# Routing constants moved into the attention, the block table beside the digit search, the list written out, expert weights prepared one half ahead

## The chip, the cores and the metric

One core of one Trainium2 chip runs the whole program. The metric is device time in microseconds (us) from one launch to its end, the median of three runs. The engines are named as the profile names them: PE (TensorE), DVE (VectorE), ACT (ScalarE), POOL (GpSimd) and SP (SyncE, which only issues DMAs here).

## What is computed

The input x has 16 batches of 512 tokens with 256 values each. An attention layer with 8 heads comes first, then a mixture of experts. Cut to what matters here:

```python
x = x + ga * attn(layernorm(x) * (1 + ca) + sa)      # 16 x 512 x 256
h = layernorm(x) * (1 + cb) + sb
logits = h @ Wr + br                                  # 8192 tokens x 8 experts
top_vals, top_idx = top_k(logits, 2)
w = softmax(top_vals)
cap = 1280                                            # tokens that an expert takes
kv, ki = top_k(where(flat_idx == e, w_flat, -1e30), cap)   # for each expert e
tok, gate = flat_tok[ki], w_flat[ki] where valid else 0
y = gelu(h[tok] @ W1[e] + b1[e]) @ W2[e] + b2[e]      # 256 -> 1024 -> 256
out = zeros.at[tok].add(y * gate)
x = x + gb * (layernorm(out + h) * gamma + beta)
```

With the inputs given, the bias of the router outweighs the rest of the logits, so all tokens choose the same two experts. Each of these takes 1280 tokens, which is 5 blocks of 256, and 10 blocks are computed in all.

## The kernel before

Three parts follow one another. `attention` runs over the 16 batches with a hand-made order of the work of each batch (`body(b, par)` with 32 slots `n`; batches -2 and -1 are the run-in). It ends with LOGITS, 128 x 64 x 8.

`route` begins behind a barrier. POOL makes constants one after the other, each with a wait for the one before (`link`, L1103 to L1149). DVE finds the two best experts of every token (L1243 to L1268) and writes KEY; PE turns KEY into one row for each expert and sixteenth of the tokens (L1201, 4 transposes). DVE then waits for POOL's last constant before L1276. The threshold of each expert is searched in ten digits of base 8 (`digit`, L1282): DVE counts four candidates (JUNK, L1286) and ACT three (L1168), PE adds the counts over the partitions with SAME (L1206), and DVE picks the digit (L1297, L1300). Behind the digits DVE marks the chosen tokens and gives each its place in the expert's list (GT L1317 to DST L1336). It counts the blocks of each expert (L1339 to L1343), PE transposes DST (L1215), and DVE works out the table INFO of active experts, blocks and first blocks on one partition in some 20 small operations (L1348 to L1368). Only then it turns the places into row and column (D L1373 to AF L1382), for both choices of each token at once. SP reads INFO and loads W1F and W2F, 1 MB each, of the first expert (L1193, L1194).

The list itself is built in 16 steps of 8 token columns. DVE makes two one-hot tiles, OE (8 x 80) and OB (8 x 128); POOL multiplies five of the eight parts of OE by token numbers into OA (L1155), ACT the other three (L1176); PE adds OB times OA into one bank of PSUM (L1228). OE, OA and OB have two buffers, and the steps are a hardware loop of two. At the end DVE makes IDX, the list of tokens (L1398 to L1401).

`experts` runs, on each engine, a loop over the active experts and an inner one over their blocks (`each`, L1493). At its head each engine reads the number of experts, the expert, its blocks and its first block from INFO into registers. For every block POOL gathers 256 rows of `h_rows` into XG with two indirect DMAs (L1548) and scatters the result of an earlier block (L1435). PE transposes XG (L1661), DVE splits it into a high and a low part XTH and XTL (L1604, L1606), PE multiplies by W1 (`mm1`), ACT takes the GELU (L1587), DVE splits that into HH and HL, and PE multiplies by W2 (`mm2`); all products are three passes (high x high, high x low, low x high; L92 to L94). The gather of block g+1 is released by the transposes and by NEXT (L1614) of block g, and the transposes of g+1 stand behind `mm1(g, 4)` in PE's order. At the head of each expert ACT writes the high parts W1H and W2H (L1576, L1579), and DVE the low parts W1L (L1618), ahead of NEXT and the split of the tokens, and W2L (L1622) behind them. SP loads the next expert's W1F once W1L is there and its W2F once W2L is there (L1516, L1518).

`last_norm` reads the sums back, normalises and writes the output. The change only adds one wait for it on SP.

## Time and profile before

| | |
|---|---|
| median of three runs | 1386.81 us (1386.51 to 1387.3) |
| the profiled execution | 1389.0 us |
| its span, first to last instruction | 1387.2 us |
| PE busy | 1163.1 us, 84% of the span |
| DVE busy | 995.6 us, 72% |
| POOL busy | 971.6 us, 70% |
| ACT busy | 754.9 us, 54% |
| mean granted clock of PE | 0.909 of full speed |

```profile
## 2 busy tenths in 40 slices
PE   7899999999999999999999999999931164979500
PEld 5556566665656666565666656565431163979500
DVE  3888687777767777776777778676457884777596
ACT  4565666666576666657666665665413233444144
POOL 3386978878697887869788786978743066545268
PEclk9999999999999999999999999999965555999855
```

Each digit stands for 34.7 us. The first 29 or 30 are the attention, the next four the routing, the next four or so the experts, and the last three the final normalisation. How to read the rows further down: in the timeline the first column is the start in us from the span's start, the second the duration; "x8" means that eight instructions are merged, and the brackets at the end give how long the engine sat idle before and who ended that. "SPq" and "POOLq" are the queues of these engines, where instructions that are not counted as work stand.

### The profile page before, as it was taken

The numbers are of one execution on the slowest core, as the hardware profiler recorded it, in microseconds if no ns is written. First come the engines' busy times: TensorE is split into PE (matmuls) and PEld (weight loads), VectorE is DVE, ScalarE is ACT, GpSimd is POOL, SyncE is SP. The second block draws the span as 40 slices with busy tenths as digits, with TensorE's granted clock in tenths as the row PEclk, the third lists the DMA queues.
The fourth block names the chain that finished last, engine by engine and source line by source line (L and its number), as shares of the span: only waits on it lengthen the run. The fifth ranks groups of instructions, "written<-read, shape, count | busy, mean of one in ns | idle before, by whom it ended". The sixth has DMA issues, their size and how long they took to land. (4 is left out here: it accounts for less than half of the span.)

```text
span 1387.2 us, 23869 instructions
## 1 busy us (share of the span) xinstructions
PE 1163.1 (84%) x5973; PEld 783.3 (56%) x5974; DVE 995.6 (72%) x2205; ACT 754.9 (54%) x1482; POOL 971.6 (70%) x1081
## 2 busy tenths in 40 slices
PE   7899999999999999999999999999931164979500
PEld 5556566665656666565666656565431163979500
DVE  3888687777767777776777778676457884777596
ACT  4565666666576666657666665665413233444144
POOL 3386978878697887869788786978743066545268
PEclk9999999999999999999999999999965555999855
DMA  4000101011010101101010100001032013232474
GB/s 149 16 18 16 58 6 62 16 47 46 15 53 8 62 16 46 46 15 53 9 62 16 46 32 17 32 17 46 31 129 24 18 43 88 43 95 43 87 253 166
DMA packets 68477, 70.89 MB, mean 51 GB/s; under 512 B 12912, under 2 KB 64032, under 8 KB 68272
## 3 DMA queue, kind: packets, MB, share of 16 engines
q1 hardware_dynamic: 46800, 47.18, 10.7%
q10 hardware_dynamic: 16896, 16.78, 3.6%
q0 software_dynamic: 4704, 6.11, 2.9%
q8 instruction: 23, 0.38, 0.1%
q14 instruction: 54, 0.44, 0.1%
HBM read 40.35 MB, written 29.45 MB: 50 GB/s over the span
## 5 line engine op out<-in xcount | busy, mean ns | idle before, releaser
L559 ACT ACTIVATE PF<-PS 128x512 f32<-128x512 f32 x512 | 298.3, 595 | 256.8 <-PE PS L929 247.6
L821 DVE TENSOR_REDUCE NMAX<-PS 128x1 f32<-128x512 f32 x512 | 342.4, 682 | 88.0 <-PE PS L938 84.5
L472 POOL TENSOR_TENSOR SF<-SF,PF 128x512 f32<-128x512 f32 x252 | 322.0, 1300 | 14.7 <-ACT PF L559 14.5
L1010 PE MATMUL PS<-PF,V 128*64 128x512 f32 x1024 | 248.0, 605 | 0.0
L928 PE MATMUL PS<-Q,K 128*128 128x512 f32 x512 | 222.3, 434 | 2.8 <-ACT PF L559 2.8
L938 PE MATMUL PS<-K,Q 128*128 128x512 f32 x512 | 205.5, 403 | 10.6 <-DVE NMAX L821 10.2
L929 PE MATMUL PS<-Q,K 128*128 128x512 f32 x512 | 201.4, 393 | 0.0
L578 ACT ACTIVATE Q<-PS 64x512 fp32r<-64x512 f32 x256 | 151.5, 592 | 48.3 <-PE PS L94 43.3
L469 POOL TENSOR_TENSOR SF<-PF 128x512 f32<-128x512 f32 x126 | 162.0, 1301 | 19.6 <-ACT PF L559 19.6
L500 POOL TENSOR_TENSOR XL<-XF,XH 128x512 fp32r<-128x512 f32 x63 | 82.6, 1312 | 128.5 <-ACT XH L633 128.4
L928 PEld LDWEIGHTS PS<-Q,K 128*128 128x128 f32 x512 | 96.5, 188 | 120.5 <-ACT PF L559 54.6
L668 DVE STREAM_TRANSPOSE XF<-PS 128x512 f32<-128x512 f32 x64 | 45.9, 717 | 119.4 <-PE PS L1028 119.4
L1010 PEld LDWEIGHTS PS<-PF,V 128*64 128x64 f32 x1024 | 62.1, 136 | 110.2 <-issue 93.9
L938 PEld LDWEIGHTS PS<-K,Q 128*128 128x128 f32 x512 | 96.4, 189 | 46.1 <-DVE NMAX L821 21.3
L929 PEld LDWEIGHTS PS<-Q,K 128*128 128x128 f32 x512 | 96.8, 189 | 10.6
L789 DVE TENSOR_TENSOR Q<-PS,Q 64x512 fp32r<-64x512 f32 x128 | 87.5, 683 | 3.7 <-ACT Q L578 1.6
L1587 ACT ACTIVATE HF<-PS,B 128x256 f32<-128x256 f32 x80 | 38.0, 474 | 81.4 <-PE PS L94 69.2
L92 PE MATMUL PS<-GH,XH 128*128 128x256 f32 x256 | 75.8, 296 | 3.5 <-DVE YT L796 2.1
L1155 POOL TENSOR_TENSOR OA<-OE,TOK 128x400 fp32r<-128x400 f32 x16 | 26.7, 1668 | 70.1 <-DVE OE L1390 70.1
L93 PE MATMUL PS<-GL,XH 128*128 128x256 f32 x256 | 72.0, 281 | 0.0
L94 PE MATMUL PS<-GH,XL 128*128 128x256 f32 x256 | 72.0, 281 | 0.0
L1028 PE MATMUL PS<-SF,ONE 128*64 128x512 f32 x252 | 64.8, 592 | 0.0
(327 smaller groups left out, 2519.7 us busy)
## 6 DMA issues: line engine op xcount, KB each, us to landing
X<-in_L_attn_x SPq DMA_DIRECT2D x16, 512.0 KB, 3.4
MODB<-mod_rows SPq DMA_DIRECT2D x16, 512.0 KB, 3.7
h_rows<-H ACTq DMA_DIRECT2D x16, 512.0 KB, 3.0
acc_rows<-H ACTq DMA_DIRECT2D x16, 512.0 KB, 4.1
out_x<-X SPq DMA_DIRECT2D x16, 512.0 KB, 2.9
A<-acc_rows SPq DMA_DIRECT2D x15, 512.0 KB, 8.8
W1F<-in_L_ffn_W SPq DMA_DIRECT2D x3, 1024.0 KB, 4.9
W2F<-in_L_ffn_W SPq DMA_DIRECT2D x3, 1024.0 KB
```

The source lines that it names most:

```text
L92: eng.matmul(out, lhs[0], rhs[0], start=first, stop=False)
L469: s_sum.done(pool.tensor_tensor(total, PF[:, u % 8 - 2, :], tile, ALU.add))
L472: s_sum.done(pool.tensor_tensor(total, total, tile, ALU.add))
L500: s_xlo.done(pool.tensor_tensor(XL[:, p, :], XF[:, :], XH[:, p, :].bitcast(F32), ALU.subtract))
L559: s_exp.done(act.activation(PF[:, u % 8, :], st_bank(u), ACT.Exp))
L578: s_qhi.done(act.activation(Q1[half * R:(half + 1) * R, 2 * idx + odd, :], bank[odd * R:(odd + 1) * R, :], ACT.Copy))
L789: s_qlo.done(dve.tensor_tensor(Q2[0:R, h, :], bank[odd * R:(odd + 1) * R, :], Q1[odd * R:(odd + 1) * R, h, :].bitcast(F32), ALU.subtract))
L821: s_mred.done(dve.tensor_reduce(NMAX[:, p % 2, r:r + 1], mx_bank(u), AX.X, ALU.max, negate=True))
L928: pe.matmul(st_bank(u), K1[:, kp, keys], Q1[:, h, :], start=True, stop=False)
L929: s_st.done(pe.matmul(st_bank(u), K2[:, kp, keys], Q2[:, h, :], start=False, stop=True))
L938: s_mx.done(pe.matmul(mx_bank(u), Q1[:, h, c * P:(c + 1) * P], K1[:, kp, :], start=True, stop=True))
L1010: last = pe.matmul(num_bank(p)[odd * R:(odd + 1) * R, :], V1[:, vp, c, :], PF[:, k % 8, :], start=(c == 0), stop=(c == TC - 1))
```

## The change

- `routing_constants` holds nearly all of POOL's constants. POOL runs it in the attention, in slot 20 of batch -1, before any addition of exponentials. LOWER, ECOLI and ECOL are made by DVE in the attention too (`same_expert`). In `route` POOL makes only ONES, ZT, ZP and BEFORE, and DVE waits for them ahead of KEY.
- The block table is worked out beside the digits: ACT counts the tokens of each expert with one Sign over HI, PE, POOL and ACT make the table on all 128 partitions in small operations, and DVE copies it to INFO in digit 6. POOL's first scatter comes behind the table.
- Behind the digits ACT's Sign takes the place of GT, and RANK (sign and running count in one) lets one comparison with a count give SEL and its sum, so that the addition and the reduction behind SEL go.
- The places are turned into row and column for the first choice of each token first; the work for the second choice (`second`) stands between the first six steps of the list. The steps are written out. ACT copies IOT into PSUM, and OE and OB read it there.
- ACT makes W1H (in two halves) and W2H of the first expert before the list, and of the next one at the end of the last block. DVE makes the first half of W1L before `s_list`, or at the end of an expert's last block, and the second half behind the split of the tokens. PE waits for that half before `mm1(g, 4)`.
- SP waits for the first gather before it loads the second expert's weights. POOL reads the table before it waits for IDX.

```diff
@@ -471,8 +489,58 @@
                     s_sum.wait(pool, b, 2 * (TC - 1) * p + 2 * (c - 2) + odd)
                     s_sum.done(pool.tensor_tensor(total, total, tile, ALU.add))
 
+            def routing_constants():
+
...
+                    n[0] += 1
+                    pool.wait_ge(s_rc, n[0])
+                f32 = dict(allow_small_or_imprecise_dtypes=True)
+                RANK8, IOT, SPARE, TOK1, NEED, NBLEV = (m[x] for x in ("RANK8", "IOT", "SPARE", "TOK1", "NEED", "NBLEV"))
+                LEVEL, STEP, MOVE = (m[x] for x in ("LEVEL", "STEP", "MOVE"))
+                link(pool.iota(RANK8[:, :], pattern=[[-1, E]], base=E, channel_multiplier=0, **f32))
+                link(pool.iota(ECOLI, pattern=[[0, 1]], base=0, channel_multiplier=1))
...
+                for j, blocks in enumerate((0, 0, 2, 3, 4)):
+                    link(pool.memset(NBLEV[:, j:j + 1], float(2 * blocks * BLK - NT)))
+                for d in range(NDIG):
+                    link(pool.tensor_scalar(STEP[:, d, :], SIGN, weight(d), None, ALU.mult))
+                    link(pool.tensor_scalar(LEVEL[:, d, :], COUNT, weight(d), None, ALU.mult))
...
                 for n in range(UNITS):
+                    if isinstance(b, int) and (b, n) == (-1, 20):
+                        routing_constants()
...
+                mask(dve.scalar_tensor_tensor(out=m["LOWER"][:, :], in0=DIFF, scalar=float(P), in1=m["SAME"][:, :],
+                                              op0=ALU.is_gt, op1=ALU.mult))
+                dve.wait_ge(s_rc, 2)
+                mask(dve.tensor_scalar(ECOLI, ECOLI, E - 1, None, ALU.bitwise_and))
+                mask(dve.tensor_scalar(m["ECOL"][:, :], ECOLI, float(CAP), float(-1 - BIG), ALU.mult, ALU.add))
...
+        pool.memset(ONES[:, :], 1.0).then_inc(s_pool, 1)
         pool.memset(ZT[:, :], 0.0).then_inc(s_pool, 1)
         pool.memset(ZP[:, :], 0.0).then_inc(s_pool, 1)
-        pool.memset(ONES[:, :], 1.0).then_inc(s_pool, 1)
-        assert n[0] + 4 == POOL_CONSTS
-        pool.iota(DIFF[:, :], pattern=[[1, P]], base=P, channel_multiplier=-1).then_inc(s_pool, 1)
+        pool.wait_ge(s_pool, ZEROS)
+        pool.memset(BEFORE[:, :], 1.0).then_inc(s_pool, 1)
+        pool.wait_ge(s_pool, ZEROS + 1)
+        pool.affine_select(out=BEFORE[:, :], in_=BEFORE[:, :], compare_op=ALU.is_gt, fill=0.0, base=0,
+                           pattern=[[1, P]], channel_multiplier=-1).then_inc(s_pool, 1)
...
+        pool.wait_ge(s_nba, 1)
+        pool.tensor_scalar(OVER[:, :], NBLEV[:, :], TOTAL[:, :], LOW8[:, :], ALU.is_lt, ALU.mult).then_inc(s_nbp, 1)
+        pool.wait_ge(s_nba, 3)
+        pool.tensor_scalar(PICK[:, :], IOT[:, 0:E], PRIOR[:, 0:1], OVER[:, 0:1], ALU.is_equal, ALU.mult).then_inc(s_nbp, 1)
+        pool.tensor_scalar(LASTB[:, :], BLOCKS[:, :], -1.0, None, ALU.add).then_inc(s_nbp, 1)
+        pool.wait_ge(s_nbp, 3)
+        for j, which in enumerate((PIDX, LASTB, FIRSTB)):
...
+        pool.tensor_scalar(TABLE[:, 3 * E + 1:3 * E + 2], BLOCKS[:, :], 1.0, None, ALU.mult).then_inc(s_nbp, 1)
         first_scatter(pool, m)
...
+        act.activation(iot_ps, IOT[:, :], ACT.Copy).then_inc(s_iot, 1)
...
+        act.wait_ge(s_split, 1)
+        act.wait_ge(s_pool, POOL_CONSTS)
+        act.activation(SGN[:, :], HI[:, :], ACT.Sign, bias=ONES[:, 0:1], accum_out=ASG[:, :]).then_inc(s_asg, 1)
+
+        def blocks(d):
+
+            if d == 1:
+                act.wait_ge(s_nbt, 1)
+                act.activation(TOTAL[:, :], asg_ps, ACT.Copy).then_inc(s_nba, 1)
+            if d == 2:
+                act.wait_ge(s_nbt, 2)
+                act.activation(PRIOR[:, :], prior_ps, ACT.Copy, accum_out=FIRSTB[:, :]).then_inc(s_nba, 1)
+                act.activation(JUNKB[:, :], OVER[:, :], ACT.Copy, accum_out=BLOCKS[:, :]).then_inc(s_nba, 1)
+
...
+        act.activation(SGN[:, :], LOW[:, :], ACT.Sign, bias=CAND[:, NDIG % 2, 0:1], scale=-1.0, accum_out=CNT[:, 1:2]).then_inc(s_sgn, 1)
+        high_weights_1(act, m, 0)
+        high_weights_2(act, m, 0)
+        for j in range(STEPS):
+            act.wait_ge(s_oe, j + 1)
+            for r in range(RPOOL, RING):
+                act.activation(OA[:, j % 2, r, :], OE[:, j % 2, r, :], ACT.Copy,
+                               scale=tok[:, j * RING + r:j * RING + r + 1]).then_inc(s_oact, 1)
...
+            if d == 5:
+                pe.wait_ge(s_nbp, 8)
+                pe.wait_ge(s_nba, 3)
+                pe.matmul(table_ps, ONES[:, :], TABLE[:, :], start=True, stop=True).then_inc(s_nbt, 1)
...
-        dve.wait_ge(s_pool, 1)
...
+        dve.wait_ge(s_pool, POOL_CONSTS)
         for q in range(TC):
             dve.scalar_tensor_tensor(out=KEY[:, q, :, :], in0=EQ[:, q::TC, :], scalar=-1.0, in1=OH1[:, q::TC, :],
                                      op0=ALU.add, op1=ALU.add).then_inc(s_key, 1)
-        dve.wait_ge(s_pool, POOL_CONSTS)
...
+            if d == 6:
+                dve.wait_ge(s_nbt, 3)
+                dve.tensor_copy(m["INFO"][:, :], table_ps[0:1, :]).then_inc(s_info, 1)
...
-        link(dve.tensor_scalar(GT[:, :], LOW[:, :], thr, None, ALU.is_gt, ALU.add, accum_out=CNT[:, 1:2]))
...
+        dve.wait_ge(s_sgn, 1)
+        link(dve.tensor_tensor(CNT[:, 3:4], CNT[:, 2:3], CNT[:, 1:2], ALU.add))
...
+        link(dve.scalar_tensor_tensor(out=RANK[:, :], in0=SGN[:, :], scalar=FAR, in1=SCAN[:, :], op0=ALU.mult, op1=ALU.add))
...
-        link(dve.tensor_tensor(SEL[:, :], SEL[:, :], GT[:, :], ALU.add))
-        link(dve.tensor_reduce(CNT[:, 3:4], SEL[:, :], AX.X, ALU.add))
+        link(dve.tensor_scalar(SEL[:, :], RANK[:, :], CNT[:, 4:5], None, ALU.is_le, ALU.add, accum_out=CNT[:, 5:6]))
...
-        dve.wait_ge(s_nb, 1)
-        eid, nb, cum, act_, cua, z = (NBR[:, j, :] for j in range(6))
-        link(dve.tensor_copy(eid, IOT[0:1, 0:E]))
-        link(dve.tensor_scalar(act_, nb_ps[0:1, :], 0.0, None, ALU.is_gt))
...
-        link(dve.tensor_copy(m["INFO"][:, :], TABLE[:, :]))
-        dve.sem_inc(s_info, 1)
...
+        def second(j):
+
+            if j == 0:
+                link(dve.tensor_tensor(EQ[:, :, :], by_tok, by_expert(D12[:, 0, :]), ALU.is_equal))
+            elif j == 1:
+                link(dve.scalar_tensor_tensor(out=EQ[:, :, :], in0=EQ[:, :, :], scalar=float(BIG), in1=by_tok,
+                                              op0=ALU.mult, op1=ALU.add))
+            elif j == 2:
+                link(dve.tensor_reduce(D12[:, 1, :], EQ[:, :, :], AX.X, ALU.min))
+            elif j == 3:
+                to_integers(1)
+            elif j == 4:
+                to_places(1)
+            elif j == 5:
+                to_floats(1)
...
+        to_integers(0)
+        to_places(0)
+        to_floats(0)
+        dve.wait_ge(s_iot, 1)
+        for j in range(STEPS):
+            dve.wait_ge(s_mm, j + 1)
+            dve.tensor_tensor(OE[:, j % 2, :, :], iot_ps[:, 0:SLOTC].unsqueeze(1).broadcast_to([P, RING, SLOTC]),
+                              af[:, j * RING:(j + 1) * RING].unsqueeze(2).broadcast_to([P, RING, SLOTC]), ALU.is_equal).then_inc(s_oe, 1)
+            dve.tensor_tensor(OB[:, j % 2, :, :], iot_ps.unsqueeze(1).broadcast_to([P, RING, P]),
+                              bf[:, j * RING:(j + 1) * RING].unsqueeze(2).broadcast_to([P, RING, P]), ALU.is_equal).then_inc(s_ob, 1)
+            second(j)
+
+        low_weights_1(dve, m, 0, 0)
...
+def half_of_inner(j):
+
+    return slice(j * (F // 2), (j + 1) * (F // 2))
+
+
+def high_weights_1(act, m, a):
+
+    m["s_w1"].wait(act, a, 0)
+    for j in range(2):
+        cols = half_of_inner(j)
+        m["xs"]["w1h"].done(act.activation(m["W1H"][:, :, cols], m["W1F"][:, :, cols], ACT.Copy))
+
+
+def high_weights_2(act, m, a):
+
+    m["s_w2"].wait(act, a, 0)
+    m["xs"]["w2h"].done(act.activation(m["W2H"][:, :, :], m["W2F"][:, :, :], ACT.Copy))
+
+
+def low_weights_1(dve, m, a, j):
+
+    cols = half_of_inner(j)
+    m["xs"]["w1h"].wait(dve, a, j)
+    m["xs"]["w1l"].done(dve.tensor_tensor(m["W1L"][:, :, cols], m["W1F"][:, :, cols], m["W1H"][:, :, cols].bitcast(F32), ALU.subtract))
...
+        sp.wait_ge(s_gx.sem, 16 * BT)
         with sp.Fori(0, nact) as a:
 
             e = sp.value_load(INFO[0:1, bass.ds(a + 1, 1)], min_val=0, max_val=E - 1)
             k_row, f_row = sp.snap(e * KC), sp.snap(e * FC)
 
-            s_w1l.wait(sp, a, 0)
+            s_w1l.wait(sp, a, 1)
...
-        pool.wait_ge(m["s_idx"], 1)
-        each(pool, None, block, block)
+
+        def first(e, a, g):
+
+            pool.wait_ge(m["s_idx"], 1)
+
+        each(pool, first, block, block)
...
+        def last(e, a, g, k):
+
+            block(e, a, g, k)
+            high_weights_1(act, m, a + 1)
+            s_m2.wait(act, g, FC - 1)
+            act.activation(DUMMY[:, 0:1], IDENT[:, 0:1], ACT.Copy)
+            high_weights_2(act, m, a + 1)
+
+        each(act, None, block, last)
...
         def expert(e, a, g):
-            s_w1h.wait(dve, a, 0)
-            s_w1l.done(dve.tensor_tensor(W1L[:, :, :], W1F[:, :, :], W1H[:, :, :].bitcast(F32), ALU.subtract))
             next_gates(e, g)
             split_tokens(g)
+            low_weights_1(dve, m, a, 1)
             s_w2h.wait(dve, a, 0)
...
+            else:
+                low_weights_1(dve, m, a + 1, 0)
...
+                if f == FC // 2:
+                    s_w1l.wait(pe, a, 1)
                 mm1(g, f)
...
+        nact = sp.value_load(m["INFO"][0:1, 3 * E:3 * E + 1], min_val=1, max_val=E)
+        m["xs"]["w2h"].wait(sp, nact, 0)
```

## Rows read from the trace of the kernel before

**Rows 1.** Stretches, whole chip: us, busy of PE, PEld, DVE, ACT, POOL, then PEclk, DMA.

```profile
0.00:1030.00 1030.00, 996.13 (x4800) 623.35 (x4801) 737.57 (x1534) 626.12 (x1201) 794.21 (x847) 0.99 0.12 37
...
1110.00:1153.00 43.00, 30.83 (x129) 28.70 (x130) 32.91 (x32) 13.85 (x48) 26.69 (x16) 0.50 0.09 32
```

**Rows 2.** Timeline, start of the routing: start, us, engine, line, operation, idle before.

```profile
1030.60 0.69 DVE L1243 TENSOR_REDUCE M<-LOGITS 128x64 f32<-128x512 f32 x1 [0.50 <-POOL RANK L1110]
...
1044.04 1.11 PE L1201 MATMUL PS<-IDENT,KEY 128*128 128x128 f32 x4 [14.17 <-DVE KEY L1268]
...
1048.57 0.69 DVE L1276 TENSOR_SCALAR BITS<-PS 128x512 uint32<-128x512 uint32 x1 [4.58 <-POOL DIFFr L1149]
```

**Rows 3.** Timeline, between the last digit and the list.

```profile
1091.42 0.75 DVE L1318 TENSOR_SCALAR_CACHE_REDUCE EQT<-LOW,CAND 128x512 f32<-128x512 f32 x1
...
1099.12 0.74 DVE L1341 SCALAR_TENSOR_TENSOR CNT<-PS,CNT 128x1 f32<-128x1 f32 x4
...
1100.24 1.12 PE L1215 MATMUL PS<-IDENT,DST 128*128 128x128 f32 x4 [2.57 <-DVEq L1344]
...
1105.55 0.69 DVE L1373 TENSOR_REDUCE D<-PS 128x64 f32<-128x512 f32 x1 [0.15 <-DVE INFO L1368]
...
1110.19 0.82 DVE L1390 TENSOR_TENSOR OE<-IOT,AF 128x640 f32<-128x640 f32 x1 [0.47 <-DVE AF L1382]
```

**Rows 4.** Timeline, one step of the list, and the first instruction behind the last.

```profile
1115.17 0.90 DVE L1390 TENSOR_TENSOR OE<-IOT,AF 128x640 f32<-128x640 f32 x1 [0.49 <-PE PS L1228]
...
1115.99 1.21 DVE L1393 TENSOR_TENSOR OB<-IOT,BF 128x1024 fp32r<-128x1024 f32 x1
...
1116.25 1.67 POOL L1155 TENSOR_TENSOR OA<-OE,TOK 128x400 fp32r<-128x400 f32 x1 [0.86 <-DVE OE L1390]
...
1118.16 1.93 PE L1228 MATMUL PS<-OA,OB 128*128 128x80 f32 x8 [0.61 <-POOL OA L1155]
...
1153.50 0.24 DVE L1398 SCALAR_TENSOR_TENSOR LF<-PS,SPARE 128x80 f32<-128x80 f32 x1 [3.41 <-PE PS L1230]
```

**Rows 5.** Groups of instructions, the last stage: POOL additions of 512.

```profile
L1850 POOL TENSOR_TENSOR X<-X,A 128x512 f32<-128x512 f32 x32 | 39.3, 1264 | 1.1 <-DVE A L1796 1.1
```

**Rows 6.** The chain in order of time, behind the list: start, us, what.

```profile
1154.70 0.52 POOLq L1491
...
1157.50 0.03 POOLq L1502
```

**Rows 7.** Timeline, the first gather.

```profile
1160.35 2.89 POOL L1548 DMA_INDIRECT XG<-h_rows,TOKN  x1 [0.30 <-issue]
...
1162.58 0.38 SPq L1516 DMA_DIRECT2D W1F<-in_L_ffn_W  x1
...
1167.99 1.11 PE L1661 MATMUL PS<-IDENT,XG 128*128 128x128 f32 x4 [14.23 <-DMA XG<-h_rows,TOKN]
```

**Rows 8.** A gather in the middle of an expert: its instruction, and a stretch with PEclk, DMA.

```profile
1220.24 1.12 POOL L1548 DMA_INDIRECT XG<-h_rows,TOKN  x1 [0.30 <-issue]
...
1222.00:1223.00 1.00, 0.96 (x8) 0.86 (x8) 0.87 (x3) 0.04 (x1) 0.18 (x2) 1.00 0.49 135
```

**Rows 9.** Timeline, the second gather.

```profile
1171.66 2.32 POOL L1548 DMA_INDIRECT XG<-h_rows,TOKN  x1 [0.30 <-issue]
...
1173.29 0.37 SPq L1518 DMA_DIRECT2D W2F<-in_L_ffn_W  x1
...
1178.45 0.65 PE L1661 MATMUL PS<-IDENT,XG 128*128 128x128 f32 x4 [2.36 <-DMA XG<-h_rows,TOKN]
```

**Rows 10.** Timeline, between the two experts.

```profile
1236.29 2.29 DVE L1618 TENSOR_TENSOR W1L<-W1F,W1H 128x2048 fp32r<-128x2048 f32 x1 [2.02 <-ACT W1H L1576]
...
1238.51 0.17 DVE L1614 COPY NEXT<-XG 128x2 f32 x1
...
1247.80 0.65 PE L1661 MATMUL PS<-IDENT,XG 128*128 128x128 f32 x4 [1.32 <-DMA XG<-h_rows,TOKN]
```

**Rows 11.** Timeline, POOL in the first batch of the attention.

```profile
50.26 2.53 POOL L469 TENSOR_TENSOR SF<-PF 128x512 f32<-128x512 f32 x2 [19.63 <-ACT PF L559]
```

## What was predicted, and how

> **What bounds the kernel now.** I read the stretches first. Up to 1030 us PE is busy for 996 of 1030 us at a granted clock of 0.99 [rows 1]: that part is bound by PE, and the change touches it at one place only. Behind it no engine is full. In the list, from 1110 to 1153, PE, DVE, POOL and ACT are busy for 31, 33, 27 and 14 of 43 us, and the clock is 0.50, which is 1.2 GHz [rows 1]. There time goes by a chain from engine to engine, so I read the timeline link by link, and at each idle bracket ask what ended it. Five places stand out. DVE sits 4.58 us until POOL's last constant [rows 2]. The table stands between PE's transposes, which end at 1101.36, and D at 1105.55 [rows 3]. OE takes another 4.64 us from D [rows 3]. POOL reads the table from 1154.70 to 1157.50, behind the list [rows 6]. And the first gather takes 7.64 us, from its second instruction at 1160.35 to PE at 1167.99 [rows 7].
>
> **The sum** is made against the profiled execution (span 1387.2 us, 1389.0 with what lies around it). The median of the three runs, 1386.81, is what I take the saving from; nothing in the change touches the 2 us between the two.
>
> **Start of the routing.** DVE's first instruction waited 0.50 us for RANK [rows 2], and would start with the barrier, some 0.2 earlier; 0.1 more for operations that POOL's no longer disturb: +0.3. PE's four transposes start at 1044.04 and take 1.11 us [rows 2]. BITS could then start at 1045.25 where it started at 1048.57: +3.3. POOL has only five fills and a selection left, beside 14 us of DVE's work, so no wait takes its place.
>
> **The constants' new place.** In rows of before they take POOL about 17 us, and seven small ones are added: 18 at the most. POOL is idle for 19.63 us up to 50.26 [rows 11], and stands there. Cover 19.6, cost 0. If it overran, the additions of batch 0 would start that much late, with gaps of several us behind them. DVE's three small operations in batch 0 cost 0 to 0.7; I take 0, since PE bounds there.
>
> **The digits.** ACT gets one Sign ahead of its three of digit 0, and small copies behind digits 1 and 2; DVE's four counts are longer than ACT's three, so 0 to 0.1 shows. The new waits: PE waits for POOL's OVER behind digit 1, with digit 2's product queued behind it (due some 3 us later); PE waits for the table in digit 5 and DVE for INFO in digit 6, with all the rest of the search behind it. POOL's eight small operations (0.2 to 0.3 us each) end some 10 us before. 0. The copy of INFO lies where DVE waits for PE.
>
> **Behind the digits.** Ahead of the transposes three 512-wide operations go (GT, the addition, the reduction), each like EQT 0.75 [rows 3] and 0.78 with its gap: 2.3. Eight tiny ones go, at 0.19 each (four CNT take 0.74 [rows 3]): 1.5. RANK comes (0.78), CNT's addition with its wait for ACT's Sign 0.3: net +2.75. Behind the transposes the table goes: D follows them by 0.1, not by 4.19: +4.1. Together **+6.9** (6.5 to 7.2, as the wait for ACT turns out).
>
> **Places.** From D to OE 4.64 us [rows 3]. Three 512-wide operations of 0.72 leave it (2.2), the five conversions are half as wide (0.4), and the loop's entry, 0.47 idle before OE [rows 3], shrinks to 0.15: **+2.9**.
>
> **The list.** Two buffers tie step j+2 to step j. OE starts at 1115.17, POOL at 1116.25 (+1.08), takes 1.67, PE starts at 1118.16 and ends 1.93 later, and DVE follows after 0.13 [rows 4]: 5.06 for two steps, 2.53 each, and 43.3 us from the first OE to LF at 1153.50 [rows 3, 4]. POOL's OA is 400 wide. In the last stage 512 take 1.264 [rows 5], so 400 would take 1.05; there DVE's multiplications take an operand from PSUM, here both inputs of OB, which runs over OA, lie in SBUF [rows 4]. With IOT in PSUM, OA costs between 1.05 and 1.67. I take 1.05, the nearest row being the one whose DVE reads PSUM. The chain is then 4.47 for two steps. The second choice adds 0.72 to DVE in steps 0 to 2 and 0.2 to 0.4 in steps 3 to 5, where DVE (OE 0.82, OB 1.21) becomes the bound: the seventh OE starts at 15.2 us, the last at 35.1, LF at 40.0. **+3.3**; with OA at 1.67 it is -0.2. The first half of W1L, 1.2 us, stands in front of LF, where DVE sat 3.41 us [rows 4]: 0.
>
> What speaks against it: the Trainium skill (VectorE: DVE Perf Modes, the section on the TRN2 errata) gives an operation from PSUM 120 fixed cycles where one from SBUF has 58. By that each OE would be 0.065 us longer, an estimate from that page that takes 0.5 from this term. The trace does not show it: a reduction of 512 takes 0.69 from SBUF and from PSUM [rows 2, 3]. The relief of OA agrees with the skill (SBUF — State Buffer, Who interferes with whom): a DVE operation with two SBUF inputs contends with a GpSimd one that reads SBUF.
>
> **The table, read early.** POOL's loads from 1154.70 to 1157.50 [rows 6] move to where it waits for the list (2.7 us idle there): **+2.8**. The loads of the other engines stay behind the list but end before the gather lands.
>
> **The first gather.** Its second instruction took 2.89 us beside DVE's W1L; one in mid-expert takes 1.12, and the rows of data move from 1222 to 1223, so that it lands about 3 us after its start at 1220.24 [rows 7, 8]. Here W1F's megabyte was also issued at 1162.58, ahead of the data [rows 7]. Both go: W1L's first half lies in the list, its second behind the split, and SP waits for the gather. 7.64 becomes 3.1: **+4.5** (0 if the time is the gather's own). ACT's W1H and W2H, 3.8 us, lie ahead of the first OE, where ACT had nothing to do.
>
> **The second gather** is where something comes back. Its second instruction, 2.32 us, ended after W2L, and it landed 5.16 us behind W2F's issue at 1173.29 [rows 9]. Now 1.2 us of W1L's second half (half of 2.29 [rows 10]) stand ahead of W2L, W2F is issued 1.2 later with W1F just before it. The landing moves by 1.2 to 1.5, and PE, which waits for it, too: **-1.3**.
>
> **Between the experts.** W1L, 2.29, stood ahead of NEXT, the split and the next gather [rows 10]; it now runs in the shadow of the last GELUs and products, so NEXT comes 2.1 earlier. But PE then waits for the gather of the next block again, to 1247.80 [rows 10], and that lands behind W2F, whose issue comes only 1.1 earlier, with W1F closer ahead: **+0.7** (0.3 to 2.8).
>
> **Ends.** The half of W1L in the last block ends when YS is due: -0.1. W2H's copy on ACT ends before SP's wait for the scatters.
>
> Sum: 0.3 + 3.3 + 6.9 + 2.9 + 3.3 + 2.8 + 4.5 - 1.3 + 0.7 - 0.1 = **23.3**; 1386.8 - 23.3 = **1363.5**.
>
> **Rivals.**
> 1. POOL slips its descriptors in between the half of W1L and W2L. Both later gathers then land 5.4 us behind W1F, as the first one did [rows 7], ahead of W2F: +0.9 in place of -1.3, and +2.8 in place of +0.7, 4.3 us better: 1359.2. For it: the second gather's instruction starts just before that half ends. Against: the two stand back to back, and all three stretched instructions ended 0.9 after DVE's. The skill (SBUF — State Buffer, the same section) would get there by another way: it infers that a tensor_tensor does not stall descriptors. The 2.89 against 1.12 us beside one says otherwise [rows 7, 8].
> 2. POOL is not relieved: OA stays 1.67, the list 43.5: 1367.0.
> 3. The first gather's time is its own, not W1F's or W1L's: 1368.0. Against it stands the 3 us of rows 8.
> 4. PE, with shorter gaps in the list, is granted its full clock; DVE then bounds at 2.05 a step over the last ten: 1.9 better, 1361.6. Against: 31 of 43 us busy left it at 0.50 [rows 1].
> 5. Slower: OE and OB are slowed by reading PSUM while PE writes there. If both took twice as long, a step would be 4.1, the list 68.5: 1392.0. It decides from 3.7 us a step. Against: D from PSUM at 0.69 [rows 3].
> 6. The change does not do what it says: the table is late, and DVE waits in digit 6. It would need POOL's eight operations to take 10 us more; under 0.02.
>
> **How the numbers follow.** Forecast 0.44 (its own range 1361 to 1366), rival 1 0.20, rival 2 0.13, rival 3 0.07, rival 4 0.08, rival 5 and 6 0.03; 0.05 for small terms adding up one way. From 1358.5 to 1368.5 leaves out rival 5 and the far ends. A measurement tells 0.2%, 2.8 us, from no change. Faster 0.96, same 0.01, slower 0.03.
>
> **What would show it.** BITS 0.1 behind the transposes; D 0.1 behind the next ones; OA at 1.05 and steps of 2.24; POOL's gather instruction 0.5 us behind IDX and PE's transposes 3 us behind the second one; the second gather at more than 5 us after W2F; NEXT without W1L ahead. The prediction is wrong if OA stays at 1.67, if the first gather still takes 7 us, or if the attention, 1030 us now, moves by more than 1.

## The result, and the profile after

| | before | after |
|---|---|---|
| median, four runs each | 1387.05 us (1386.51 to 1389.3) | 1362.74 us (1360.75 to 1365.21) |
| ratio after / before | | 0.9818, 95% interval 0.98 to 0.9836 |
| the profiled execution, its span | 1387.2 us | 1359.7 us |
| mean granted clock of PE | 0.909 | 0.917 |

The change saves 24.3 us by the medians, and 27.5 us between the two profiled executions. The slices of the changed kernel, PE and its granted clock:

```profile
PE   7899999999999999999999999999972175989400
...
PEclk9999999999999999999999999999985556999755
```

Read from start to start of named instructions in both timelines, the span splits as follows (the last column is the prediction's term for that stretch; a positive difference is time saved):

| from ... to | before | after | saved | predicted |
|---|---|---|---|---|
| start ... last LOGITS | 1029.91 | 1025.35 | 4.56 | 0 |
| ... PE's transposes of KEY | 14.13 | 13.81 | 0.32 | 0.3 |
| ... BITS | 4.53 | 1.15 | 3.38 | 3.3 |
| ... GT or EQT (ten digits) | 42.06 | 41.70 | 0.36 | 0 |
| ... D | 14.92 | 7.97 | 6.95 | 6.9 |
| ... first OE | 4.64 | 1.62 | 3.02 | 2.9 |
| ... LF (the list) | 43.31 | 36.35 | 6.96 | 3.3 |
| ... transposes of gather 1 | 14.49 | 6.87 | 7.62 | 2.8 + 4.5 |
| ... of gather 2 | 10.46 | 14.47 | -4.01 | -1.3 |
| ... of gather 3 | 11.97 | 14.19 | -2.22 | 0 |
| ... of gather 6 (next expert's first) | 44.39 | 45.08 | -0.69 | 0 |
| ... of gather 7 | 12.99 | 10.49 | 2.50 | 0.7 |
| ... last YS | 54.81 | 55.81 | -1.00 | 0 |
| ... end | 84.59 | 84.84 | -0.25 | -0.1 |

The timeline of the changed kernel where the routing turns into the list answers to [rows 2 to 4]: start, us, engine, line, operation, and in brackets the idle time before it and what ended it.

```profile
1040.31 0.69 DVE L1343 TENSOR_SCALAR BITS<-PS 128x512 uint32<-128x512 uint32 x1 [1.21 <-PE PS L1262]
...
1088.83 1.11 PE L1286 MATMUL PS<-IDENT,DST 128*128 128x128 f32 x4 [1.77 <-DVEq L1402]
...
1089.98 0.69 DVE L1437 TENSOR_REDUCE D<-PS 128x64 f32<-128x512 f32 x1 [1.26 <-PE PS L1286]
...
1103.52 0.82 DVE L1444 TENSOR_TENSOR OE<-PS,AF 128x640 f32<-128x640 f32 x1
1104.25 1.22 DVE L1446 TENSOR_TENSOR OB<-PS,BF 128x1024 fp32r<-128x1024 f32 x1
...
1104.42 0.86 POOL L1199 TENSOR_TENSOR OA<-OE,TOK 128x400 fp32r<-128x400 f32 x1 [1.21 <-DVE OE L1444]
...
1127.95 0.24 DVE L1452 SCALAR_TENSOR_TENSOR LF<-PS,SPARE 128x80 f32<-128x80 f32 x1 [1.38 <-PE PS L1298]
```

BITS is released by PE, not by POOL. D starts right behind the transposes. POOL's OA takes 0.86 us where it took 1.67 [rows 4], and LF still waits 1.38 us with half of W1L ahead of it. Then the two gathers, POOL's and SP's side ([rows 7, 9] before):

```profile
1130.54 1.04 POOL L1630 DMA_INDIRECT XG<-h_rows,TOKN  x1 [0.44 <-issue]
1131.89 0.97 POOL L1630 DMA_INDIRECT XG<-h_rows,TOKN  x1 [0.30 <-issue]
...
1134.51 1.63 POOL L1517 DMA_INDIRECT acc_rows<-YS,TOKS  x1 [0.52 <-issue]
1136.45 1.59 POOL L1517 DMA_INDIRECT acc_rows<-YS,TOKS  x1 [0.30 <-issue]
...
1137.63 3.48 POOL L1625 COPY TOKN<-IDX 128x2 uint32 x1
...
1137.66 1.22 DVE L1510 TENSOR_TENSOR W1L<-W1F,W1H 128x1024 fp32r<-128x1024 f32 x1
...
1138.81 2.28 DVE L1702 TENSOR_TENSOR W2L<-W2F,W2H 128x2048 fp32r<-128x2048 f32 x1
...
1139.07 0.38 SPq L1598 DMA_DIRECT2D W1F<-in_L_ffn_W  x1
...
1141.26 0.37 SPq L1600 DMA_DIRECT2D W2F<-in_L_ffn_W  x1
...
1142.96 1.11 POOL L1630 DMA_INDIRECT XG<-h_rows,TOKN  x1 [0.30 <-issue]
...
1149.29 0.47 PE L1743 MATMUL PS<-IDENT,XG 128*128 128x128 f32 x1 [5.79 <-DMA XG<-h_rows,TOKN]
```

The first gather is short now: instructions of 1.04 and 0.97 us, transposes at 1134.82. The second is where something came back. TOKN, a copy of two words per partition that takes 0.19 us elsewhere, takes 3.48 us, as long as DVE's half of W1L (1137.66 to 1138.88) and W2L (1138.81 to 1141.09) last. Only then do the gather's instructions start, and their rows land 5.2 us after the last one ended (1144.07 to 1149.29), where the first gather's needed 1.96 (1132.86 to 1134.82) and the second gather's in the kernel before 4.5 (1173.98 to 1178.45, [rows 9]). PE idles for 5.79 us, and the clock that it gets afterwards is the low one (windows of the changed kernel; busy of PE, PEld, DVE, ACT, POOL, then PEclk, DMA):

```profile
1149.30:1154.00 4.70, 4.70 (x22) 4.70 (x23) 0.36 (x2) 0.47 (x1) 0.25 (x1) 0.50 0.29 33
1154.00:1163.50 9.50, 9.50 (x81) 9.50 (x80) 6.67 (x21) 4.33 (x8) 5.93 (x11) 0.99 0.18 34
```

22 matmuls in 4.7 us at 1.2 GHz, 81 in 9.5 us at 2.4 GHz: the 2.22 us of the block behind the second gather.

### The profile page after: what moved, and what is told of

Read it like the earlier page. It is cut to its first block and busy times, and to the rows that moved or that the text cites. A ratio compares the mean times of both kernels' runs of the same rounds, so it can differ in the third digit from the quotient of the medians.

```text
span 1359.7 us, 23684 instructions
## 1 busy us (share of the span) xinstructions
PE 1163.7 (86%) x5975; PEld 786.6 (58%) x5976; DVE 989.6 (73%) x2189; ACT 757.9 (56%) x1494; POOL 958.7 (71%) x1096
## 5 line engine op out<-in xcount | busy, mean ns | idle before, releaser
L559 POOL TENSOR_TENSOR NLO<-NF,NHI 128x512 fp32r<-128x512 f32 x32 | 41.2, 1289 | 32.5 <-DVE NHI L878 32.5
```

## The experiments

All are compared by the same stretches. Times in us; "LOGITS to YS" is everything that the change aims at, without the attention, whose length differs from execution to execution (below).

| kernel | to LOGITS | list | LF to gather 1 | 1 to 2 | 2 to 3 | 3 to 4 | 6 to 7 | LOGITS to YS | ratio to before |
|---|---|---|---|---|---|---|---|---|---|
| before | 1029.91 | 43.31 | 14.49 | 10.46 | 11.97 | 11.90 | 12.99 | 272.70 | |
| before_iot_psum | 1028.50 | 35.60 | 14.43 | 10.22 | 11.98 | 11.91 | 12.91 | 264.42 | 0.9941 |
| before_sp_waits | 1029.71 | 43.31 | 11.60 | 13.07 | 14.18 | 11.92 | 12.73 | 274.32 | 1.0013 |
| changed kernel | 1025.35 | 36.35 | 6.87 | 14.47 | 14.19 | 12.08 | 10.49 | 249.51 | 0.9818 |
| constants_late | 1026.00 | 36.34 | 7.13 | 13.30 | 13.60 | 12.15 | 10.33 | 253.89 | 0.9857 |
| list_sbuf | 1026.18 | 44.11 | 6.82 | 14.39 | 13.83 | 12.07 | 10.43 | 256.72 | 0.9864 |
| pe_wait_once | 1028.24 | 36.34 | 6.80 | 15.70 | 14.66 | 12.09 | 10.42 | 251.03 | 0.9812 |
| half_moved | 1028.88 | 36.34 | 6.87 | 12.46 | 13.37 | 12.07 | 10.38 | 246.53 | 0.9799 |
| clear_first | 1027.47 | 36.34 | 6.83 | 12.18 | 13.55 | 12.09 | 10.38 | 246.43 | 0.9797 |
| beside_gather | 1026.73 | 36.33 | 8.48 | 11.49 | 12.06 | 12.09 | 10.32 | 245.84 | 0.9791 |
| loads_behind_second | 1028.82 | 36.34 | 6.82 | 11.14 | 13.03 | 12.09 | 9.34 | 243.89 | 0.9783 |
| clear_and_behind | 1028.94 | 36.33 | 6.87 | 10.40 | 12.97 | 12.09 | 9.22 | 243.00 | 0.9781 |
| moved_320 | 1025.60 | 36.33 | 6.86 | 13.23 | 14.03 | 11.94 | 10.33 | 246.46 | 0.9792 |
| joined | 1027.18 | 36.34 | 6.89 | 10.37 | 12.80 | 11.93 | 9.92 | 241.94 | 0.9766 |

Each row comes from one profiled execution. The column "1 to 2" has two parts: how long after the first transposes POOL's last instruction of the second gather ended, and how long after that its rows let PE start. "PE idle" is PE's wait for the second gather, "clock" the lowest granted clock in that wait and the block behind it.

| kernel | instruction ends | rows behind it | PE idle | clock |
|---|---|---|---|---|
| before | 5.99 | 4.47 | 2.36 | 1.00 |
| before_iot_psum | 5.98 | 4.24 | 1.79 | 1.00 |
| before_sp_waits | 8.42 | 4.66 | 3.81 | 0.50 |
| changed kernel | 9.26 | 5.22 | 5.79 | 0.50 |
| constants_late | 9.24 | 4.05 | 4.45 | 0.50 |
| list_sbuf | 9.24 | 5.15 | 5.00 | 0.50 |
| pe_wait_once | 9.24 | 6.46 | 6.34 | 0.50 |
| moved_320 | 9.25 | 3.97 | 3.98 | 0.50 |
| half_moved | 8.31 | 4.14 | 2.97 | 0.50 |
| clear_first | 8.58 | 3.60 | 3.78 | 0.50 |
| beside_gather | 6.44 | 5.05 | 2.94 | 1.00 |
| loads_behind_second | 9.25 | 1.90 | 2.00 | 1.00 |
| clear_and_behind | 8.44 | 1.95 | 1.12 | 1.00 |
| joined | 8.41 | 1.95 | 0.96 | 1.00 |

The first part repeats within 0.02 us in the five kernels whose edits don't touch this place (changed kernel, constants_late, list_sbuf, pe_wait_once, moved_320). The second part runs from 3.97 to 6.46 us in the same five. So a difference of 1 us in "1 to 2" between two kernels tells something only where it lies in the first part, or where the rows come in under 2 us.

**constants_late: where the attention's 4.6 us come from.** 44 constants back in `route`, on POOL ahead of its fills, and one more wait of DVE ahead of KEY:

```diff
@@ route, POOL
+        link(pool.iota(SPARE[:, :].rearrange(...), ...))
...
+            link(pool.tensor_tensor(MOVE[:, first:last, :], MOVE[:, first:last, :], LEVEL[:, first + 1:last + 1, :], ALU.add))
         pool.memset(ONES[:, :], 1.0).then_inc(s_pool, 1)
@@ route, DVE
         dve.wait_ge(s_pool, POOL_CONSTS)
+        dve.wait_ge(s_late, NLATE)
```

> The changed kernel, with 44 of its 50 constants on POOL put back behind the attention, where the kernel before had them. Theory A (the attention ran 4.6 us shorter by a variation from execution to execution, not by the change): the attention's length in the trace (start of the span to the first routing instruction) varies between 1025 and 1030 us whatever the constants' place, and the kernel is slower by the wait for the last constant alone, about 3.3 us, so 1366.0 us against 1362.7. Theory B (the constants in POOL's early idle time are what shortened it): the attention is back at 1030 us, POOL idles for some 19 us again before its first addition, and the kernel takes 1362.7 + 3.3 + 4.6 = 1370.6 us.

Measured: 1367.12 us (1365.82 to 1368.68), ratio 0.9857 (0.9838 to 0.9876), and an attention of 1026.00. Theory B is out: POOL's early constants don't shorten the attention. Putting them late cost 5.7 us in the stretch to KEY, not 3.3, since DVE now waits for them ahead of KEY (5.74 us idle) and POOL's four fills and its selection stand behind them too; over LOGITS to YS it is 4.4, because the second gather's rows landed 1.2 us sooner in this execution and the block behind them was 0.6 shorter. But theory A holds only in part. Over all fourteen traces the attention is 1028.5 to 1029.9 in the three with the code of before and 1025.4 to 1028.9 in the eleven with the code of after. Taken apart, two things lie in it.

The first is in the start, and both codes have both forms. PE's 16 products at 22.7 us take 3.68 us in one form and 1.94 in the other (3.44 or 3.55 where only some are slow; timeline, the profiled execution of before, then that of after):

```profile
22.72 3.68 PE L882 MATMUL PS<-X 64*64 64x256 f32 x16 [1.18 <-ACT X L543]
```

```profile
22.19 1.94 PE L955 MATMUL PS<-X 64*64 64x256 f32 x16 [1.18 <-ACT X L611]
```

The trace's records of the clock begin between 19.9 and 21.9 us, at full speed, in the seven executions with the short form (before_iot_psum among them), and between 25.9 and 27.1 us in the seven others. That the long form is the lower of the two levels is read from the durations; no record of the clock covers it. POOL's first SF follows at 47.2 to 48.8 us after the short form, and at 49.4 to 50.6 after the long one. The profiled execution of before (50.26) had the long form, that of after (47.20) the short one: 3.06 of the 4.56 us are that, and no part of the change.

The second is the change's, though nobody meant it. From the twelfth batch's LOGITS to the thirteenth's, where the attention's hardware loop is left, the three traces with the code of before take 62.1 to 62.4 us and those with the code of after 60.7 to 61.0. The waits in that stretch, DVE's and PE's, before and then after (us in total, times, longest):

```profile
DVE GATE L641 <- issue: 1.8, 1, 1.8
...
PE PS L928 <- ACT PF L559: 0.8, 1, 0.8
```

```profile
DVE YT L869 <- issue: 0.8, 2, 0.5
...
PE PS L1011 <- DVE NMAX L894: 0.5, 1, 0.5
```

In before DVE stands 1.84 us ahead of GATE at 860.66 with nothing to wait for; POOL then waits 1.33 us for DVE's MV, ACT 2.77 for POOL's NB where it waits 1.43 after, and PE 0.82 for ACT's PF. After, that pause is not there. What differs for DVE is where its code lies: the change puts three instructions ahead of the loop. That a pause belongs to the place of the code is argued from this and was not tried by itself.

**list_sbuf and before_iot_psum: the list.** The same part undone in the changed kernel, and done alone in the one before:

```diff
@@ list_sbuf
-            dve.tensor_tensor(OE[:, j % 2, :, :], iot_ps[:, 0:SLOTC]...
+            dve.tensor_tensor(OE[:, j % 2, :, :], IOT[:, 0:SLOTC]...
-            dve.tensor_tensor(OB[:, j % 2, :, :], iot_ps...
+            dve.tensor_tensor(OB[:, j % 2, :, :], IOT[:, :]...
```

> The changed kernel, with OE and OB reading the ramp IOT from SBUF again (its copy in PSUM is not read). Theory A (POOL's OA was slowed by DVE's operation with two SBUF inputs): OA goes from 0.86 back to 1.67 us, and the list from the first OE to LF from 36.3 to 43 us, 6.5 to 7 us more in all. Rival (the list is shorter because it is written out and D's second half moved): OA stays at 0.86 and the list at 36 to 37 us.

```diff
@@ before_iot_psum
+        act.activation(iot_ps, IOT[:, :], ACT.Copy).then_inc(s_iot, 1)
-                dve.tensor_tensor(OE[:, par, :, :], IOT[:, 0:SLOTC]...
+                dve.tensor_tensor(OE[:, par, :, :], iot_ps[:, 0:SLOTC]...
-                dve.tensor_tensor(OB[:, par, :, :], IOT[:, :]...
+                dve.tensor_tensor(OB[:, par, :, :], iot_ps...
```

> The kernel before, with one part of the change alone: IOT copied to PSUM and read from there by OE and OB; the list stays a loop. Theory A (contention): OA 0.86 instead of 1.67 us, the loop's pair of steps 4.25 instead of 5.06 us, the list 36.5 instead of 43.3 us and the whole 1380.2 instead of 1387.0 us. My forecast's value for OA would give 1.05, 4.47 and 38.2 us. Rival (written-out steps are what matters): no change, 1387.

Measured: 1368.45 us for the first, with OA at 1.77 us and the list at 44.11, 7.8 us more; 1379.1 us for the second (ratio 0.9941, 0.9919 to 0.9962), with OA at 0.86 and the list at 35.60, 7.7 us less. OA of list_sbuf, then of before_iot_psum (duration in ns: least, median, most):

```profile
L1199 POOL TENSOR_TENSOR OA<-OE,TOK x16: 1763/1770/1772, 1093.3 to 1132.2; 128x400 fp32r<-128x400 f32 x16
```

```profile
L1156 POOL TENSOR_TENSOR OA<-OE,TOK x16: 855/857/857, 1109.8 to 1140.8; 128x400 fp32r<-128x400 f32 x16
```

So the copy of IOT in PSUM is more than the whole gain, and DVE gets it too: in list_sbuf OE takes up to 1.48 us, in before_iot_psum 0.82 each time. That OE from PSUM is no longer than the shortest from SBUF (0.82 us in the kernel before) also answers the 0.5 us that the prediction held against this term. In before_iot_psum, without the second choice's six operations among the steps, the list is 0.75 us shorter than in the changed kernel: there the first six steps take 14.1 us, 2.2 more than six later ones, while a later step takes 1.99 us where the loop of before_iot_psum has 2.08. PE's waits in the list, in before and in the changed kernel (us in total, times, longest), show that POOL has left the chain:

```profile
PE PS L1228 <- POOL OA L1155: 19.0, 15, 10.5
```

```profile
PE PS L1296 <- DVE OB L1446: 6.0, 10, 2.9
```

 The Trainium skill (SBUF — State Buffer, Who interferes with whom) has the rule: a DVE operation with two SBUF inputs contends with a GpSimd one that reads SBUF. The trace agrees: OA takes 1.77 us in list_sbuf and 1.67 in before, against 0.86 us in before_iot_psum and in the changed kernel.

**before_sp_waits: what held the first gather, and what comes of it.** One wait of SP in the kernel before:

```diff
         nact = actives(sp)
+        sp.wait_ge(s_gx.sem, 16 * BT)
         with sp.Fori(0, nact) as a:
```

> The kernel before, with one part of the change alone: SP waits for the first gather to land before it asks for the next expert's W1F. W1L still stands beside the gather's instructions, so the second one still takes 2.9 us. Theory A (both W1F ahead of the rows of data and W1L hold the first gather): PE's transposes come 5 us after that instruction's start where it was 7.64, and the kernel gains 2.6 us (1384.4). Rival B (W1L alone, by the late second instruction): the 7.64 us stay within 0.3 and the time at 1387.0. Rival C (W1F alone): 3 us from start to transposes, 4.5 us gained.

Measured at the place in question: transposes 4.75 us behind the second instruction's start (1160.17 to 1164.92) where it was 7.64 [rows 7], 2.9 us gained; theory A, and both causes share the 4.5 us of the prediction. Measured at the end: 1390.31 us, ratio 1.0013 (1.0 to 1.0026). The gain went within two blocks. The split came earlier, so W2L came ahead of POOL's next TOKN and not beside its gather:

```profile
1167.76 2.29 DVE L1623 TENSOR_TENSOR W2L<-W2F,W2H 128x2048 fp32r<-128x2048 f32 x1
1167.85 2.43 POOL L1544 COPY TOKN<-IDX 128x2 uint32 x1
...
1170.22 0.37 SPq L1519 DMA_DIRECT2D W2F<-in_L_ffn_W  x1
...
1172.34 0.99 POOL L1549 DMA_INDIRECT XG<-h_rows,TOKN  x1 [0.30 <-issue]
```

and the gather's last instruction ended 8.42 us behind the first transposes instead of 5.99; from there its rows took about as long as before (4.66 against 4.47 us). The second transposes came at 1177.99, 0.46 earlier than before, with PE idle for 3.81 us instead of 2.36, and the block after that took 14.18 us instead of 11.97. One edit of before shows the changed kernel's two losses, 2.6 and 2.2 us, in small.

**half_moved, clear_first, beside_gather: POOL behind DVE's weights.** In all three DVE's part of the first expert is written out, and W1L's second half is made in the list. In clear_first DVE then waits until POOL has issued the first gather (the wait on s_tok) and makes W2L while the rows are on the way; beside_gather leaves that wait out; half_moved makes W2L behind split_tokens, as the changed kernel does. (The first expert can stand ahead of a loop that starts at 1, since every token takes two experts and two are always active.)

```diff
         low_weights_1(dve, m, 0, 0)
+        low_weights_1(dve, m, 0, 1)
@@ clear_first, ahead of DVE's loop over the experts
+        def first_expert(e):
+            s_tok.wait(dve, 0, 1)
+            s_w2h.wait(dve, 0, 0)
+            s_w2l.done(dve.tensor_tensor(W2L..., W2F..., W2H..., ALU.subtract))
+            next_gates(e, 0)
+            split_tokens(0)
```

> The changed kernel, with DVE's part of the first expert written out: W1L's second half is made in the list, right behind the first, and W2L when POOL has issued the first gather, while its rows are on the way; nothing of the weights is left behind the first split. Theory A (the second gather came late, 14.47 us behind the first, because POOL's TOKN was held up by W1L and W2L, and PE's idle time of 5.79 us then cost it its full clock, 2.2 us in the next block): the transposes of the second gather come 8.7 to 9.5 us behind those of the first, the next ones 12.1 behind them, and the kernel takes 1355.7 us against 1362.7. Rival B (POOL is late by its own two scatters, 1.6 us each, that stand ahead of TOKN): second transposes 12 to 13 us behind, the clock falls still, 1361. Rival C (the early W2L delays the list, the gather or the split): first transposes 1 to 2 us later, which eats part of the gain.

> As clear_first, but W2L stays behind the first split, where the changed kernel has it; only W1L's second half is moved into the list. Theory A (POOL's small TOKN waits until W2L is through): W2L starts 1.2 us earlier, POOL's second gather with it, so that the second transposes come 13.2 us behind the first instead of 14.47; PE's clock still falls, the next ones come 14.2 later; 1361.5 us. Rival (W1L's half was what POOL waited for): 10 to 11 us and no fall of the clock, 1357.

> As clear_first, without DVE's wait for POOL's issue: W2L, 2.29 us, starts right behind IDX and runs beside POOL's first gather instructions. Theory A (a DVE operation with two SBUF inputs holds POOL's descriptor writing, as 2.89 against 1.12 us in the kernel before): one gather instruction takes 1.7 to 2.9 instead of 1.0 us, ends 0.9 behind W2L, and the first transposes come 0.8 to 1.5 us later than in clear_first. Rival, by the Trainium skill, SBUF — State Buffer, Who interferes with whom (a tensor_tensor does not stall descriptors): 1.0 to 1.1 us each and transposes at the same time or 0.3 earlier.

Measured: 1361.09, 1361.13 and 1359.92 us; from LOGITS to YS 3.1, 3.0 and 3.7 us less than in the changed kernel. The move of W1L's half costs the list nothing. In clear_first TOKN waits for no weight of DVE's any more (0.72 us), but POOL's two scatters stand ahead of it (1138.70 1.63, 1140.64 1.59), so that the gather's last instruction ends at 1145.45, and its rows land 3.6 us later. The expectation of 8.7 to 9.5 us failed at 12.18, and rival B gave 12 to 13, the fall of the clock and 1361 us. Why the scatters stand there the theories did not say: W2L, moved beside POOL's work, now holds a small copy ahead of them,

```profile
1135.25 2.30 POOL L1615 TENSOR_TENSOR TOKP<-TOKG,NOUGHT 128x2 uint32<-128x2 uint32 x1
```

and the first scatter starts 1.83 us behind the first transposes where it started 0.31 ahead of them in the changed kernel. The rest is the next expert's loads, two megabytes asked for at 1137.76 and 1138.40, which were not among the theories either. half_moved, with its TOKN at 2.44 us, has the gather's instruction 0.95 us earlier, near the 1.2 expected; the other 1.1 of its 2.0 us lie in the landing of the rows, which varies that much by itself. beside_gather, where POOL's scatters lie as in the changed kernel and no weight is left behind the split, has the instruction at 6.44 us instead of 9.26 and its TOKN at 0.78: so 2.8 us are what W1L's half and W2L cost POOL behind the first split. It also answers the dispute on descriptors:

```profile
1132.70 2.29 DVE L1707 TENSOR_TENSOR W2L<-W2F,W2H 128x2048 fp32r<-128x2048 f32 x1 [2.31 <-issue]
...
1133.26 2.58 POOL L1631 DMA_INDIRECT XG<-h_rows,TOKN  x1 [0.30 <-issue]
```

A gather instruction that takes 0.97 us in clear_first takes 2.58 beside W2L and ends 0.85 behind it, and the first transposes come 1.65 us later (0.8 to 1.5 expected). The Trainium skill (SBUF — State Buffer, Who interferes with whom) infers that a tensor_tensor does not stall descriptors; the measurement says that the gather's instruction is held beside this one, with both inputs in SBUF.

**loads_behind_second and clear_and_behind: SP's loads.**

```diff
@@ experts, SP's loop
+            g0 = sp.value_load(INFO[0:1, bass.ds(a + 2 * E, 1)], min_val=0, max_val=E * MAXB)
+            s_gx.wait(sp, g0 + 1, 0)
             s_w1l.wait(sp, a, 1)
             s_w1.done(sp.dma_start(W1F[:, :, :], ...))
```

> The changed kernel, with one more wait of SP: the next expert's W1F and W2F are asked for when the second gather of the expert has landed, not when the first has. Theory A (in the changed kernel the rows of the second gather, whose last instruction ended at 1143.96, lay behind W1F and W2F, a megabyte each, and landed 5.3 us later, where the first gather's rows land 1.9 us behind their instruction): the second transposes come at 11.1 us behind the first instead of 14.47, PE idles 2.4 instead of 5.79 us, and the block behind them takes 12.1 to 13.4 instead of 14.19; at the boundary, where the loads lay in the gather's way too, 9.5 instead of 10.49. Together 1357 us against 1362.7. Rival B (POOL's late instructions alone make it late, the loads don't matter): 14.2 to 14.5 us and 1362.7.

> clear_first and loads_behind_second together: no half of a weight is made by DVE between the first split and POOL's second gather, and SP's loads stay behind that gather's rows. Theory A (clear_first gained only 2.3 us at this place because the rows then lay behind the loads: 3.6 us from the last instruction's end to the transposes instead of 1.9): second transposes 10.5 us behind the first, the next ones 12.1 behind them, boundary 9.5: 7.1 us less than the changed kernel in these stages, 1355.6 us. Rival B (the two remedies are one and the same): no better than the better of the two alone.

Measured: 1358.47 us (1356.47 to 1359.9), ratio 0.9783 (0.9769 to 0.9797), and 1358.06 us, 0.9781 (0.9768 to 0.9795). With one wait of SP, and TOKN held up as before (3.41 us), the second transposes come 11.14 us behind the first, as expected (11.1), PE idles for 2.00 us, and at the boundary 9.34 takes the place of 10.49 (9.5 expected):

```profile
1141.10 3.41 POOL L1627 COPY TOKN<-IDX 128x2 uint32 x1
...
1146.36 1.11 POOL L1632 DMA_INDIRECT XG<-h_rows,TOKN  x1 [0.30 <-issue]
...
1149.37 0.66 PE L1745 MATMUL PS<-IDENT,XG 128*128 128x128 f32 x4 [2.00 <-DMA XG<-h_rows,TOKN]
...
1149.51 0.38 SPq L1600 DMA_DIRECT2D W1F<-in_L_ffn_W  x1
```

So of the 14.47 us in the changed kernel 3.3 were the rows' place behind W1F and W2F; against the other four kernels with the same loads it is 2.1 to 4.6. Clearing DVE's weights out of the way on top of it brings 0.8 more in the instruction's end (10.40 in all), which the medians do not tell apart. The block behind it takes 13.0 in both, not 12.1, though PE has its full clock there. The loads, it seems, now stand in the way of the scatters (not tried by itself): in clear_and_behind, loads_behind_second and joined DVE waits 1.90 to 1.95 us at YS until an earlier scatter has landed, where no other kernel here waits more than 0.11 us in that block, and PE then waits 0.66 to 0.71 us for DVE's HL behind it:

```profile
1158.62 0.88 DVE L1741 SCALAR_TENSOR_TENSOR YS<-PS,GATES,YB 128x256 f32<-128x256 f32 x2 [1.90 <-DMA acc_rows<-YS,TOKS]
...
1160.21 0.39 PE L100 MATMUL PS<-W2H,HH 128*128 128x256 f32 x1 [0.66 <-DVE HL L1720]
```

The last 0.2 us stay open.

**pe_wait_once and moved_320: why every block is 0.17 us longer.**

```diff
@@ pe_wait_once
             for f in range(LEAD):
+                if f == LEAD - 1:
+                    s_w1l.wait(pe, a, 1)
                 mm1(g, f)
@@ block
-                if f == FC // 2:
-                    s_w1l.wait(pe, a, 1)
```

> The changed kernel, with PE's wait for the second half of W1L moved from the middle of every block to the third first product of every expert. Theory A (this wait, against a register's value, is what makes a block 12.07 us long where it was 11.90): blocks are back at 11.90, over 8 of them 1.3 us, 1361.4 us; the boundary may lose up to 0.5 of it. Rival B (it lies elsewhere, in code or addresses): blocks stay at 12.07 and the time within 0.3 us of the changed kernel's 1362.7.

```diff
@@ moved_320
+    sb("PAD", [P, 80])
     XG = sb("XG", [P, BT, D + E])
```

> The changed kernel, with 320 bytes left free in SBUF ahead of XG, so that XG, the split tokens, HF, HH and HL lie against the weights as in the kernel before, up to multiples of 512 bytes; no instruction is changed. Theory A (a matmul every 120.0 ns instead of every 116.6 comes of where PE's two operands lie): a steady block takes 11.90 instead of 12.07 us, 1.6 us over ten blocks, 1361.1 us. Rival B (it comes from elsewhere): 12.07 and no change.

Measured: 1363.15 us with blocks of 12.07 to 12.09, so PE's wait is not the cause; its second gather took 1.2 us more, all of it in the landing of the rows. With the 320 free bytes 1359.32 us, ratio 0.9792 (0.9775 to 0.981), and blocks of 11.91 to 11.96 us. These are two runs, and their ratio can't be told from the changed kernel's 0.9818 (0.98 to 0.9836); the blocks are what shows the effect, and 1.2 us of what this kernel gained over the changed one lie in the landing of the second gather's rows, not in the blocks. One kind of product in a steady block, in the changed kernel and then in moved_320 (busy us, mean ns of one):

```profile
L101 PE MATMUL PS<-XTL,W1H 128*128 128x256 f32 x17 | 4.8, 283 | 0.0
```

```profile
L101 PE MATMUL PS<-XTL,W1H 128*128 128x256 f32 x17 | 4.7, 278 | 0.0
```

Before had 278 too. No instruction differs between these two kernels, only where XG and the tiles behind it lie. Theory A: the change moved these tiles against the weights, and that is 1.5 of the 1.7 us that the blocks gave back (the stretches of gather 3 to 6 and gather 7 to YS take 44.57 and 54.86 us). Why some distances cost PE 3 ns in 117 the runs don't tell.

**joined: what comes of all of it.** clear_and_behind, and in it:

```diff
@@ experts
+    sb("PAD", [P, 80])
     XG = sb("XG", [P, BT, D + E])
```

> clear_and_behind together with moved_320: the weights' low halves out of the second gather's way, SP's loads behind that gather, and the 320 bytes that shift the tokens' tiles. Theory (the address effect is a rate of PE's own and adds to the rest): from the last LOGITS to the last YS 6.5 us less than in the changed kernel by the first two, 2.2 less by blocks of 11.92 instead of 12.07, together 240.8 us where the changed kernel has 249.5; 1354.1 us against 1362.7. Rival (a shorter block lets another engine's wait show: ACT or DVE, which hand HF and HL over within a block): blocks between 11.95 and 12.07, 1355 to 1356 us.

Measured: 1355.32 us (1354.52 to 1358.03), ratio 0.9766 (0.9752 to 0.978) against 0.9818 for the changed kernel; 241.94 us from LOGITS to YS, with blocks of 11.88 to 11.93. It is faster than both the kernel before and the changed one; from clear_and_behind, at 0.9781 (0.9768 to 0.9795), the ratios do not tell it apart. The blocks are the theory's, the time is the one that the rival gave. The boundary took 9.92 where clear_and_behind had 9.22, which is most of what is missing from the 240.8 expected.

## Why the prediction was right, and where its steps were not

The time was forecast at 1363.5 and measured at 1362.74. That it came so near is luck, as the last paragraph of this section adds up. Most steps hold within 0.2 us: the start of the routing (0.32 against 0.3), the wait for BITS (3.38 against 3.3), the constants in POOL's idle time (0), the part behind the digits (6.95 against 6.9), the places (3.02 against 2.9), the table read early (from LF to the start of the second gather instruction 6.85 became 3.94, 2.9 against 2.8), the first gather (7.64 became 2.93, 4.7 against 4.5), the ends (-0.25 against -0.1). What they have in common: each was a sum of instructions whose rows stood in the trace, and the one that follows was named. The ten digits gave 0.36 where 0 was said; 0.29 of it is the copy of HI, 0.43 us in all eleven traces with the code of after and 0.71 or 0.72 in the three with the code of before; no run tells why. The prediction counted five fills of POOL's at the start of the routing where there are four, which changed nothing.

**The list** was mis-sized: 6.96 against 3.3. The relief of OA came, but its value was wrong: 0.86 us, where 1.05 was taken from POOL's additions in the last stage [rows 5]. That row was chosen as free of the contention, and was not shown to be; and scaled by width its 1.264 us give 0.99, not 1.05 (the chain of two steps would then be 4.4, not 4.47). The sum also had the wrong path: it kept POOL in the chain, but at 0.86 PE waits for OB and no longer for OA, and a pair of steps is OE 0.82, OB 1.14 and PE 1.95, 3.97 us, 1.99 a step where 2.24 was said. DVE's rate was mis-sized too: from one OE to the next it needs 1.87 us, its two operations overlapping, where 0.82 and 1.21 were added up. Of the 3.66 us, 1.1 lie in the first six steps (14.1 against 15.2), 2.1 in the nine behind them and 0.4 in the tail. That the contention also cost DVE (OE at up to 1.48 us, in the trace of before as in list_sbuf) stood in no term.

**The second gather** was mis-sized the other way: -4.01 against -1.3. The step that failed says that its landing moves by the 1.2 us that W1L's half takes. It left out POOL's side: the first block's two scatters, 3.5 us, which lay in the shadow of the slow first gather, now stood ahead of TOKN, so that TOKN, which in before had come 1.4 us ahead of W2L (1169.46 and 1170.83), met both W1L and W2L and took 3.48 us. The gather's last instruction ended 9.26 us behind the first transposes instead of 5.99: that is 3.27 of the 4.01 us, and beside_gather, at 6.44, puts 2.8 of it on the weights; 0.45 are left for the scatters, net of the 1.2 us by which W2L had stretched the instruction in before. The other 0.75 lie in the landing (5.22 against 4.47), less than it varies by itself. The loads behind which the rows land, 3.3 us in loads_behind_second, are thus no new loss; their cost was in the kernel before as well. The rule that the prediction used for both gathers, about 5.2 us behind W2F's issue, does not hold: it was 8.03 us here and 3.25 between the experts. Rival 1 saw POOL slip in between the two; its first small instruction did (1137.50, 1.42 us), the next one did not, and the outcome was the opposite of its 4.3 us.

**The block behind it** had no term at all, and cost 2.22: PE's clock, 0.50 in the window from 1149.30 to 1154, after 5.79 us without work. The prediction weighed the clock for the list only (rival 4, which did not come: 0.50 from 1091.60 to 1127), not for an idle time that it itself lengthened. That 2.36 us of idle time before [rows 9] had left the full clock was no proof for a longer one.

**Between the experts** 2.50 against 0.7. NEXT at 1210.42 came without W1L ahead, and the gather's instruction was no longer stretched (1.10 us instead of 2.03), so that it ended 5.74 us behind the transposes instead of 8.50: 2.76 gained. The step that failed is that the landing hangs on W2F's issue: the rows came 4.75 us behind that instruction, much as before (4.48), and W2F (1215.80) did not hold them back any further.

**The rate of the blocks**, -1.7 over all, could not be foreseen from the trace; 1.5 of it hangs on addresses (moved_320).

**The attention** was said not to move by more than 1, and a larger move was named as a sign that the prediction is wrong. Between the two profiled executions it moved by 4.56, of which 3.06 are the start's two forms and 1.14 the loop's end without DVE's pause (62.10 us against 60.96). By the spans without the start's 3.06 the saving is 24.4, as the medians have it. So the sum of 23.3 was right by errors that cancel: it had 3.7 too little for the list, 1.8 for the boundary, 1.5 for the attention without its start, and 0.9 for the digits and the small terms, 7.9 in all; it had 4.9 too much for the second gather and the clock behind it, and 1.8 for the blocks and the end, 6.8 in all. That leaves 1.1, the difference to 24.4.

## What to carry to other kernels

A wait that you shorten moves everything queued behind it: before you book the gain, follow each queue (here POOL's scatters and SP's loads) to the next place where it meets something: a small copy of POOL's, which came 1.3 us later, met two of DVE's weights and took 3.5 us instead of 0.2, and two megabytes asked for 3 to 5 us before the gather's last instruction ended held 256 rows for 2 to 4.6 us. Work that nobody needs for 50 us should be asked for behind the transfer that someone waits for now; then look at what it meets there, here the scatters. And when two engines slow each other, the uncontended time is in no row of that stage; a row of another stage is a bound only if that stage is shown to be free of it.

## What was not expected of the hardware

- GpSimd's small instructions are held as well as its descriptors while DVE runs a subtraction with both inputs in SBUF: a copy of 128x2 took 3.48 us instead of 0.19 beside two of them, and an indirect DMA instruction 2.58 instead of 0.97 beside one.
- 320 bytes of SBUF between PE's operands: a 128x128 by 256 product every 120.0 ns or about every 117 ns. The Trainium skill says that PE never waits on anyone (SBUF — State Buffer, Who interferes with whom); no run here shows who or what PE waits for, but its rate is not independent of where the operands lie.
- One engine's pause of 1.84 us with nothing to wait for, where a hardware loop is left, reached PE through POOL and ACT as 0.82 us. It is in all three traces with the code of before (1.84 to 2.03 us) and in none of the eleven with three more instructions ahead of the loop.
- Two megabytes of loads in flight held the second gather's rows back by 2.1 to 4.6 us (3.97 to 6.46 us behind the last instruction in five kernels that do not differ there, 1.90 without the loads): kernels that are alike at this place can differ there by one or two microseconds.
- PE's granted clock fell to 0.50 around the second gather in the eight traces where PE idled there for 2.97 to 6.34 us, and stayed at full in the six with 0.96 to 2.94 us. What the fall costs does not follow the length of the idle time: the block behind it took 14.18 us after 3.81 us of it and 13.60 after 4.45, where 11.97 to 12.06 us is its length at the full clock with nothing else in the way.
